# One-hots of 42 nodes a group in both graph layers, with three bf16 parts stacked in one contraction

## What is computed

```python
# layer 0, 4 heads of 32
xl = x @ W_lin.T;  x_j = xl[src]
alpha = leaky_relu((xl[dst]*att_src).sum + (x_j*att_dst).sum + (ef*att_edge).sum)
e = exp(alpha - segment_max(alpha, dst)[dst])
out = segment_sum(x_j * e / segment_sum(e, dst)[dst], dst) + bias + x
x = layernorm(x + elu(layernorm(out) * gamma + beta))
# layer 1, 8 heads of 16
q, k, v = x @ Wq.T, x @ Wk.T, x @ Wv.T
alpha = (q[dst] * w_ij * k[src]).sum(head) / 4 * cutoff
x = layernorm(x + segment_sum(alpha * v[src], dst))
```

## Time and profile before

| | |
|---|---|
| median of 3 runs | 4795.31 us |
| profiled execution | 4802.87 us |
| its span, first to last instruction | 4801.1 us |
| PE / PE weight loads | 49% / 45% busy |
| VectorE (DVE) | 51% |
| ScalarE (ACT) | 12% |
| GpSimd (POOL) | 75% |
| gathers of layer 0, first to last start | 46.2 to 2218.6 us |
| gathers of layer 1, first to last start | 2445.9 to 4744.5 us |
| data moved | 595.82 MB, mean 124 GB/s |

### The profile page before, as it was taken

How to read it: one execution, slowest core, us unless ns; L and a number is a source line. 1 busy time by engine, 2 the same in 40 slices (tenths; PEclk the granted TensorE clock), 3 DMA queues, 4 the chain that set the end, 5 groups by cost and what they waited for, 6 DMA issues and landing times. The chain is left out here.

```text
span 4801.1 us, 60860 instructions
## 1 busy us (share of the span) xinstructions
PE 2362.4 (49%) x18992; PEld 2166.5 (45%) x18992; DVE 2435.6 (51%) x3629; ACT 588.2 (12%) x893; POOL 3583.5 (75%) x3333
## 2 busy tenths in 40 slices
PE   2333334444444433335556555555555555556654
PEld 2333333333333333334345555555555555555553
DVE  2344444444444444445845555555555555555555
ACT  0111111111111111111420000000000000000002
POOL 5777777777777777773557777777777777777775
PEclk6666666666666666667677878888888787787786
DMA  7433333444444443332344444444444444444443
GB/s 166 104 103 103 100 101 101 109 111 111 111 111 111 107 112 102 101 102 54 107 148 145 142 146 142 146 141 147 143 145 144 143 146 142 146 141 147 141 146 94
DMA packets 324898, 595.82 MB, mean 124 GB/s; under 512 B 101041, under 2 KB 194257, under 8 KB 324593
## 3 DMA queue, kind: packets, MB, share of 16 engines
q0 software_dynamic: 130160, 323.05, 26.5%
q1 hardware_dynamic: 181424, 261.60, 17.1%
q10 hardware_dynamic: 13264, 10.66, 0.7%
HBM read 578.39 MB, written 16.64 MB: 124 GB/s over the span
## 5 line engine op out<-in xcount | busy, mean ns | idle before, releaser
L1157 POOL DMA_INDIRECT ring<-kv_table,den_cols x1616 | 1807.3, 1118 | 518.5 <-issue 518.2
L393 POOL DMA_INDIRECT ring<-x_table,idx x1612 | 1672.7, 1038 | 524.4 <-issue 491.1
L1197 PE MATMUL psum<-ring,work 128*128 128x128 f32 x3232 | 671.6, 393 | 925.0 <-DVE ring L1268 921.3
L1197 PEld LDWEIGHTS psum<-ring,work 128*128 128x128 f32 x3232 | 623.6, 296 | 967.6 <-issue 966.3
L1265 DVE TENSOR_TENSOR ring<-ring 128x1024 f32<-128x1024 f32 x202 | 247.5, 1225 | 871.3 <-POOLq L1169 871.3
L1204 PE MATMUL psum<-work,ring 128*128 128x128 f32 x3232 | 516.1, 327 | 39.7 <-DVE ring L1279 38.8
L1204 PEld LDWEIGHTS psum<-work,ring 128*128 128x128 f32 x3232 | 501.4, 244 | 55.0 <-DVE ring L1279 54.3
L482 PE MATMUL psum<-work 128*128 128x128 f32 x3232 | 490.5, 315 | 14.5 <-DVE work L676 14.5
L1240 ACT ACTIVATE work<-psum 128x1024 f32<-128x1024 f32 x202 | 206.9, 1024 | 2083.8 <-PE psum L1188 2083.8
L482 PEld LDWEIGHTS psum<-work 128*128 128x128 f32 x3232 | 452.6, 224 | 16.2 <-DVE work L676 16.1
L452 PE MATMUL psum<-ident_sb,score 128*128 128x128 f32 x51 | 15.5, 442 | 840.4 <-DVE score L599 840.4
(11 more groups left out here) (161 smaller groups left out, 2218.0 us busy)
## 6 DMA issues: line engine op xcount, KB each, us to landing
dst_all<-dst_row_dram SPq DMA_DIRECT2D x204, 512.0 KB
ring<-ea_dram SPq DMA_DIRECT2D x202, 512.0 KB, 4.0
ring<-kv_table,den_cols POOLq DMA_INDIRECT x1616, 2.9
ring<-x_table,idx POOLq DMA_INDIRECT x1612
ea_pair<-ea_turned_dram SPq DMA_DIRECT2D x102, 128.0 KB, 2.6
ring<-q_table SPq DMA_DIRECT2D x202, 64.0 KB, 1.8
ring<-xpad_dram SPq DMA_DIRECT2D x20, 320.0 KB, 3.4
kv_table<-ring ACTq DMA_DIRECT2D x10, 640.0 KB, 4.1
```

The costliest lines, as they stand in the source:

```text
L393: pool.indirect_dma_start(x_rows[:, h * CHUNK_TILES + t, :], None, k["x_table"], bass.IndirectOffsetOnAxis(idx[h][:, t:t + 1], 0))\
L1157: pool.indirect_dma_start(kv[j][:, t, :], None, k["kv_table"], bass.IndirectOffsetOnAxis(idx[:, tile:tile + 1], 0))\
L1197: last = pe.matmul(q_ps[j % 2][:, t * P:(t + 1) * P], onehotT[:, t * P:(t + 1) * P], q_win[j], start=True, stop=True)
```

## The change

The window of a pass is 42 nodes (`WIN`) in place of 128, so that three parts of each of 42 nodes fit on 126 partitions (`KWIN`).

- Both tables of target values are stored as (node, part, value) in bf16. 42 nodes are then 126 rows, and one bf16 product over 126 partitions adds the three parts. The turned one-hot repeats each node three times (`node_of` is `arange(128) // 3`).
- Layer 0 scores: 2 products of 512 columns a group into `dst_ps`, in which the group's four scores have rows of their own; at a chunk's end a ScalarE copy, 8 transposes and two more VectorE steps bring them to the edges' layout.
- Layer 0 denominators: fp32 products of `ex` with the fp32 one-hot. `ex_parts`, `ex_group`, `onehot_bf` and ScalarE's two copies a group go.
- Layer 1: the turned one-hot is made as in layer 0, from `dst_all` that SP loads; the 8 transposes (L1188), ScalarE's copy (L1240) and the fp32 spread go; the spread is 8 bf16 products.
- Operands move to PSUM: `iota_pass` and a copy of `ex` in layer 0; `iota_pass`, `alpha` and the intermediate product in layer 1, where q is now multiplied first.
- `q_table` is made on POOL (`split_q`, four instructions a batch) and written by SP.
- Each slot of `kv` has three semaphores in turn.

```diff
+WIN = 42
+KWIN = PARTS * WIN
...
-    q_table = nc.dram_tensor("q_table", [NODE_ROWS, FEAT], F32, kind="Internal").ap()
+    q_table = nc.dram_tensor("q_table", [NODE_ROWS, PARTS, FEAT], BF16, kind="Internal").ap()
...
+    iota_pass = k["bank"][3][:, 0:WIN]
+    ex_ps = k["bank"][3][:, P:P + HEADS0 * CHUNK_TILES].rearrange("p (h t) -> p h t", h=HEADS0)
...
             def scores_group(d, g):
...
-                for t in range(GROUP):
-                    at = (g * GROUP + t) * HEADS0
-                    for part in range(PARTS):
-                        last = pe.matmul(scores_ps[:, at:at + HEADS0], onehotT[g % 2][:, t * P:(t + 1) * P],
-                                         ai_win[g % 2][:, part * HEADS0:(part + 1) * HEADS0],
-                                         start=False, stop=False)
+                for half in range(2):
+                    last = pe.matmul(dst_ps[:, half * 512:(half + 1) * 512], ai_win[:, g * ROWS:(g + 1) * ROWS],
+                                     onehotT[g % 2][:, half * 512:(half + 1) * 512], start=False, stop=False)
...
+            def close_scores(s):
...
+                wait_here(pe, dst_copied, s + 1, pe_gate)
+                for t in range(GROUP):
+                    last = pe.transpose(dst_turned[:, t * ROWS:(t + 1) * ROWS], dst_scores[:, t * P:(t + 1) * P],
+                                        k["ident_sb"][0:ROWS, 0:ROWS])
...
             def make(u, s, tile):
-                dve.tensor_tensor(out=onehot[u], in0=k["iota_pass"].unsqueeze(1).to_broadcast([P, GROUP, P]),
+                dve.tensor_tensor(out=onehot[u], in0=iota_pass.unsqueeze(1).to_broadcast([P, GROUP, WIN]),
...
-                    in1=ex[:, :, bass.DynSlice(tile, GROUP)].rearrange("p h t -> p t h").unsqueeze(3)
+                    in1=ex_ps[:, :, bass.DynSlice(tile, GROUP)].rearrange("p h t -> p t h").unsqueeze(3)
...
+            def split_q(u, n):
+                q = qkv[u][:, :, 0:FEAT]
+                pool.wait_ge(qkv_copied, BATCH * (n + 1) + 2)
+                if n > 1:
+                    pool.wait_ge(q_out[u], 16 * (n // 2))
+                pool.tensor_copy(q_parts[u][:, :, 0, :], q)
+                for p in range(1, PARTS):
+                    pool.drain()
+                    last = pool.tensor_tensor(out=q if p < PARTS - 1 else q_parts[u][:, :, p, :], in0=q, in1=q_parts[u][:, :, p - 1, :],
+                                              op=ALU.subtract)
+                    if p < PARTS - 1:
+                        pool.drain()
+                        pool.tensor_copy(q_parts[u][:, :, p, :], q)
+                last.then_inc(q_split, 1)
...
+            for n in range(BATCHES - 2):
+                u = n % 2
+                first_power(n + 1)
+                second_power(u, n)
+                add_bias(u, n // 2 + 1)
+                take_one_off(u, n // 2 + 1)
+                if n:
+                    split_q(1 - u, n - 1)
             first_power(BATCHES - 1)
             second_power(0, BATCHES - 2)
+            split_q(1, BATCHES - 3)
             second_power(1, BATCHES - 1)
+            split_q(0, BATCHES - 2)
+            split_q(1, BATCHES - 1)
...
+                    sp.wait_ge(onehotT_made, n0 + j + 1)
+                    sp.dma_start(dst_all[j % 2], k["dst_row"][0:1, bass.DynSlice((SLOTS * i + j) * GP, GP)]
+                                 .to_broadcast([P, GP])).then_inc(dst_in[j % 2], 16)
                     sp.wait_ge(msg_made, n0 + j + 1)
-                    sp.dma_start(q_win[j], k["q_table"][bass.DynSlice(starts[j], P), :]).then_inc(q_in[j], 16)
+                    sp.dma_start(q_win[j], k["q_table"][bass.DynSlice(starts[j], WIN), :, :].rearrange("n s f -> (n s) f"))\
+                      .then_inc(q_in[j], 16)
...
+            def make_onehot(i, n, j):
+                dve.wait_ge(dst_in[j % 2], 8 * n + 16 - 8 * (j % 2))
+                dve.wait_ge(q_spread, n + 1)
+                dve.tensor_scalar(onehotT[j % 2], dst_all[j % 2][0:KWIN, :], k["base_f"][0:KWIN, bass.DynSlice(i, 1)],
+                                  k["node_pass"][0:KWIN, :], ALU.subtract, ALU.is_equal).then_inc(onehotT_made, 1)
+                dve.tensor_tensor(out=onehot[j], in0=iota_pass.unsqueeze(1).to_broadcast([P, GROUP, WIN]),
...
             def messages(i, n, j, nth):
-                dve.wait_ge(w_in[j], 16 * (nth + 1))
-                dve.wait_ge(kv_ready, n + 1)
-                dve.tensor_tensor(out=prod, in0=kv[j][:, :, 0:FEAT], in1=w[j], op=ALU.mult)
-                dve.drain()
-                dve.wait_ge(q_spread, n + 2)
-                dve.tensor_tensor(out=prod, in0=prod, in1=tiles3(q_ps[j % 2]), op=ALU.mult).then_inc(q_used, 1)
+                dve.wait_ge(kv_ready, n + 1)
+                dve.wait_ge(q_spread, n + 3)
+                q = tiles3(q_ps[j % 2])
+                dve.tensor_tensor(out=q, in0=q, in1=kv[j][:, :, 0:FEAT], op=ALU.mult)
+                dve.drain()
+                dve.wait_ge(w_in[j], 16 * (nth + 1))
+                dve.tensor_tensor(out=prod, in0=q, in1=w[j], op=ALU.mult).then_inc(q_used, 1)
```

More of the change, by code:

```diff
@@ L116, in program @@
     work = sb("work", [P, 5 * GROUP * P])
+    dst_all = [sb(f"dst_all{i}", [P, GROUP * P], I32) for i in range(2)]
     idx0 = [sb(f"idx{i}", [P, CHUNK_TILES], I32) for i in range(2)]
@@ L290, in layer0, with part @@
     GP = GROUP * P
[L291 to L295 removed]
+    cut = [0]
+    def part(cols):
+        cut[0] += cols
+        return k["work"][:, cut[0] - cols:cut[0]]
+    onehot = [part(GROUP * WIN).rearrange("p (t n) -> p t n", t=GROUP) for _ in range(2)]
+    message = [part(GP).rearrange("p (t f) -> p t f", t=GROUP) for _ in range(2)]
+    onehotT = [part(GP // 2).bitcast(BF16)[0:KWIN, :] for _ in range(2)]
+    ROWS = CHUNK_GROUPS * HEADS0
+    dst_scores = part(GP)[0:ROWS, :]
+    assert cut[0] <= 5 * GP
+    dst_all = k["dst_all"]
     ea_pair = [sb(f"ea_pair{i}", [P, 2, P]) for i in range(2)]
@@ L566, in next_pass @@
                 dve.drain()
-                for numbers in (k["node_pass"], k["iota_pass"]):
-                    dve.tensor_scalar(numbers, numbers, float(P), None, ALU.add)
+                for numbers in (k["node_pass"], iota_pass):
+                    dve.tensor_scalar(numbers, numbers, float(WIN), None, ALU.add)
                 dve.drain()
@@ L761, in between @@
     qkv = [part(3 * B).rearrange("p (b w) -> p b w", b=BATCH) for _ in range(2)]
+    q_parts = [part(3 * B // 2).bitcast(BF16).rearrange("p (b s w) -> p b s w", s=PARTS, b=BATCH) for _ in range(2)]
     rden = part(BATCH * HEADS0)
@@ L802, in between @@
     qkv_out = [S(f"qkv_out{i}") for i in range(2)]
+    q_split = S("q_split")
+    q_out = [S(f"q_out{i}") for i in range(2)]
     with nc.Block() as block:
@@ L1069, in layer1 @@
     w = [tiles3(part(GP)) for _ in range(SLOTS)]
-    q_win = [part(FEAT) for _ in range(SLOTS)]
+    q_win = [part(FEAT // 2).bitcast(BF16)[0:KWIN, :] for _ in range(SLOTS)]
     prod = tiles3(part(GP))
+    iota_pass = k["bank"][1][:, 0:WIN]
     message = [tiles3(part(GP)) for _ in range(2)]
     idx = k["idx1"]
-    alpha = part(GROUP * HEADS1)
+    alpha = k["bank"][1][:, P:P + GROUP * HEADS1]
     edge_w = part(GROUPS1 * GROUP)
     assert cut[0] <= RING_COLS - NODE_ROWS
-    onehot = [tiles3(k["work"][:, u * GP:(u + 1) * GP]) for u in range(SLOTS)]
-    onehotT = k["work"][:, 4 * GP:5 * GP]
-    sum_ps = [k["bank"][u][:, 0:P] for u in range(2)]
-    T_ps = k["wide"][0]
+    GW = GROUP * WIN
+    onehot = [tiles3(k["work"][:, u * GW:(u + 1) * GW]) for u in range(SLOTS)]
+    onehotT = [k["work"][:, SLOTS * GW + u * GP // 2:SLOTS * GW + (u + 1) * GP // 2].bitcast(BF16)[0:KWIN, :] for u in range(2)]
+    dst_all = k["dst_all"]
+    sum_ps = [k["wide"][0][:, u * 512:u * 512 + WIN] for u in range(2)]
     q_ps = [k["psum"][:, 2 * 512:4 * 512], k["wide"][1]]
@@ L1085, in layer1 @@
     idx_in = S("idx1_in")
-    kv_in = [S(f"kv_in{i}") for i in range(SLOTS)]
+    TURNS = 3
+    kv_in = [[S(f"kv_in{i}_{c}") for c in range(TURNS)] for i in range(SLOTS)]
     w_in = [S(f"w1_in{i}") for i in range(SLOTS)]
@@ L1096, in layer1 @@
     summed = S("summed1")
+    added = S("added1")
     pool_gate = S("pool1_gate")
@@ L1286, in add @@
                 dve.wait_ge(summed, n + 1)
-                window = k["sumT"][:, bass.DynSlice(start, P)]
-                dve.tensor_tensor(out=window, in0=window, in1=sum_ps[j % 2], op=ALU.add)
+                window = k["sumT"][:, bass.DynSlice(start, WIN)]
+                dve.tensor_tensor(out=window, in0=window, in1=sum_ps[j % 2], op=ALU.add).then_inc(added, 1)
             def one_round(i, groups, first, r):
@@ L1314, in _ @@
                 dve.drain()
-                dve.tensor_scalar(k["iota_pass"], k["iota_pass"], float(P), None, ALU.add)
+                for numbers in (k["node_pass"], iota_pass):
+                    dve.tensor_scalar(numbers, numbers, float(WIN), None, ALU.add)
                 dve.drain()
```

264 lines of the change are left out of this document (122 added, 142 removed).

## The result

The changed kernel takes 4518.77 us (median of 4 runs, 4516.26 to 4521.41) where the kernel before takes 4795.03: a ratio of 0.9424, 95% interval 0.9408 to 0.9440. It is faster by 276 us; forecast were 308.

What follows compares the result with a forecast made beforehand. The prediction took POOL, busy with gathers, as the bound. Its terms gave a span of 4801.1 - 249 - 110 - 5 + 56 = 4493 us, then 4493 + 1.8 - 7.6 = 4487 us, range 4400 to 4600 us.

Steps and rivals of the forecast that it cites:

- POOL is the bound, and its gathers' excess is on the path: Both layers: POOL goes from gather to gather; gather time above the median, 274 and 146 us, is all on the path.
- What holds a gather is VectorE's second SBUF input: Both layers: gathers wait for VectorE instructions reading two SBUF tensors; one input in PSUM frees them, -274 and -146 us.
- The slower rival: Both layers: any VectorE work holds gathers, so the 420 us stay and the time is 4846 us; chance 0.05.
- the -110: Layer 0: -146 us from L673 and L676 no longer holding gathers, +36 us for holds that stay.
- The turned one-hot holds for 0.56 us, met 45% of the time: 25 + 36 us: Holds left at random phase: 25 us in layer 1; 36 in layer 0, of which 11 are for the maxima.
- Gathers land late: Layer 1: extra loads delay gathers' landing past 6 us, so POOL stands 0.5 us a group, 4588 us; chance 0.05.
- The ring between the layers: Between the layers: POOL's split waits for ScalarE's table copies, making a step 18.4 us against 12.3; +56 us (37 to 80).
- After the last gather VectorE sets the time: After layer 0's last gather: casts go, a second `ex` copy is added, ten groups of sums change by -2; sum -5 us.
- From the span to the median: Whole kernel: the profiled execution is 1.8 us over its span and 7.6 over the median, so 4493 becomes 4487 us.

Runs made afterwards that it cites:

- b_q_first_2: Kernel before with only layer 1's product order changed, kv times q first, in place in PSUM, then times w: 4700.55 us, ratio 0.9803.
- a_no_hold_2: Changed kernel with both layers' turned one-hots made by a scalar_tensor_tensor that reads the node numbers from PSUM: 4462.06 us, ratio 0.9310.
- a_all_sbuf: Changed kernel with one-hot node numbers, layer 0's exponentials and layer 1's weights back in SBUF, q product still first and in PSUM: 4679.19 us, ratio 0.9763.
- a_same: The changed kernel, unaltered, run again on the second chip beside its variants: 4517.73 us, ratio 0.9427.

## Why the prediction was right, by its steps

**POOL is the bound, and its gathers' excess is on the path.** Right, but for one reading: not all idle time before the gathers of before was "issue". In layer 0 33 us of 524 were waits for VectorE, and 31 still are. The sum of the gathers' durations fell by 1807.3 - 1566.3 = 241 us in layer 1 and 1672.7 - 1571.0 = 102 us in layer 0, and the layers' stretches by 232 and 102.

**What holds a gather is VectorE's second SBUF input.** Right for the `tensor_tensor` instructions, and shown by two runs that move operands alone: one product reordered -93 us, the operands put back +160 us. The turned one-hot holds with a single tensor in SBUF (beside its two columns of scalars); in another form and with the node column in PSUM it holds nothing, -56 us. The slower rival, VectorE at work at all, would have had `b_q_first_2` at no gain and `a_no_hold_2`, whose VectorE works longer, at a loss. Where the account falls short is layer 0: the prediction puts its gain down to L673 and L676 losing one SBUF input, and gives the shorter one-hot nothing. The -102 us are near the -110, but with both inputs back in SBUF (`a_all_sbuf`) only 18 of them are lost. That the two numbers agree is partly luck: the step holds for 18 us, and the rest came with other parts of the change.

**The turned one-hot holds for 0.56 us, met 45% of the time: 25 + 36 us.** A little small. Above the medians now stand 1566.3 - 1616 x 0.946 = 37.6 us in layer 1 and 1571.0 - 1612 x 0.944 = 49.3 us in layer 0. When a gather is held is more involved than one hold from 0.25 us on. In layer 1 there are four cases, by when the gather asks: from 0.28 us before the start of L1293 to 0.10 after it, 51 gathers wait until 0.11 us after the start, 11 us in sum; from 0.11 to 0.27 us, 38 pay nothing; from 0.27 us to near the end, 82 wait for its end, 25 us; and 31 meet the end of one that had been stretched, 0.08 us each, 2 us. Inside L1293 162 gathers ask, 28 us in sum, 0.137 us a group against the 0.125 of a random phase; the 11 us of those that ask before its start had no place in the prediction. This varies from one execution to the next: in `a_same` the 28 us are 18. In layer 0 L590 takes 26 us and the maxima's scans and adds 18 us, against 25 and 11.

By the Trainium skill (SBUF — State Buffer, § Who interferes with whom) an instruction in a two-port mode holds the shared ports for its whole length. The row of 331.75 in the earlier trace rows and the cases above show otherwise: 38 gathers ask 0.11 to 0.27 us after the start and pay nothing. The same section says that a DMA which seems stalled by VectorE is one for which GpSimd is kept from generating descriptors; that fits what these gathers show, in that POOL's own instruction becomes longer, but no run tells what part of its work is held up.

**Gathers land late.** A rival at 0.05, and a small part of it came: POOL's gaps in layer 1 sum to 501 instead of 492 us, 13 of them over 0.6 us, and the gather of 3009.09 above has a DMA as what ended the idle time before it. 9 us instead of the rival's 101, at a DMA share of 0.65 where I gave 0.69.

**The ring between the layers: +6.1 us for 8 steps, +7 at the end, 56 in all.** The ring is there, every step of it in the order that was given, but shorter. In the batch shown it takes 8.8 us from the end of a second power (2232.41) to the end of the last table copy (2241.20; forecast 10.1), 4.7 for the split (5.6) and 2.7 for the two powers (2.7); the eight steps with a split are 16.6 us long on average, against 18.4. From the first second power to the last it is +38 us, from there to the first gather +2, against +49 and +7. By the Trainium skill (GPSIMD Engine Reference, § 3.1) the estimate was 4.7 us a split, of 1.39 us for each two-input instruction and 0.96 for each cast. The rows of L883 show 1.39; the cast takes 0.72, less than that. (With 4.7 us a split the term of 56 us comes to 47, not 46.)

**After the last gather VectorE sets the time, -5 us.** This step failed. It is TensorE. Stretches of the last chunk's sums, before and after, in the columns of the earlier trace rows:

```profile
2240.00:2300.00 60.00, 37.82 (x285) 33.74 (x285) 36.90 (x64) 16.27 (x26) 6.80 (x7) 0.78 0.12 35
```

```profile
2140.00:2190.00 50.00, 47.94 (x320) 45.61 (x320) 17.85 (x41) 0.62 (x1) 0.14 (x2) 0.50 0.00 1
```

```profile
2140.07 3.64 PE L505 MATMUL psum<-work 128*128 128x42 f32 x16 [3.30 <-DVE work L687]
2143.64 1.28 PE L507 MATMUL psum<-work,score 128*4 128x42 f32 x16
2144.86 3.64 PE L505 MATMUL psum<-work 128*128 128x42 f32 x16
2148.43 1.28 PE L507 MATMUL psum<-work,score 128*4 128x42 f32 x16
```

TensorE works 47.94 of 50 us, at the clock 0.50, 4.8 us a group; before, the clock of these 60 us was 0.78 in the mean, but nine of the ten groups ran at 1.00, the higher level of 2.4 GHz: there the 16 message products of three times the columns took 2.05 us, and a group 3.5.

```profile
2250.52 2.05 PE L482 MATMUL psum<-work 128*128 128x128 f32 x16 [0.54 <-DVE work L676]
```

From the first group's add to the last one's it is 43.1 us for 31.2, and VectorE waits 29 us of the 50 for TensorE's sums. I had the fp32 denominators in the sum, but at the clock of before. From the last gather to the first second power it is 104.6 instead of 93.0 us: +11.6, not -5. That the stretch came out at +51.3 as forecast is luck, two errors that cancel: 17 us too little here, 16 too much in the ring and its end.

**From the span to the median.** The profiled execution of before lay 7.6 us above the median and I carried that over; that of after lies 0.1 below its own. So of the 32 us between 4487 and 4519, 24 are the terms above (17 in layer 1, 8 in layer 0, -2 at the start, +1 at the end), and 7.6 are this.

What stays open: whether SP's queue is what keeps the nine steps between the layers above 108 us when the split is moved or shortened, what part of the change brings most of layer 0's gain, what it is in the turned one-hot that holds a gather, and what starves the engines on the first chip.

## What to carry to other kernels

Where POOL issues indirect DMAs without a break, compare their mean with their minimum: in this kernel most of the excess was time in which a VectorE instruction with two SBUF inputs ran, and in layer 1 one operand in PSUM gave it back, with no instruction fewer. Where two such instructions stand back to back, as in layer 0, shortening the first may do as much; undo the parts one at a time before you say which it was. An engine that waits in a queue ahead of the next batch's first step makes a ring of what were two pipelines; put such work a step later. And before a stretch is given to one engine, work it out at the clock that the change may bring, not at that of before.

## What the runs showed of the hardware that I had not expected

- TensorE's granted clock fell from 0.67 and 0.80 in the two stretches to 0.50, with its busy time in the first up (161 to 276 us of 400) and in the second down (293 to 225 us of 500). The message products are a third as wide and there are a third fewer matmuls in the stretch of layer 1; which of these goes with the clock no run separates.
- A third of the columns takes 3% less time at the same clock: 16 products of 42 columns take 3.64 us at 0.50, 16 of 128 columns took 3.76 where the kernel before had 0.50, and 2.03 at 1.00. The 16 weight loads beside them take 3.49 us at 0.50 in both kernels and 1.86 at 1.00, so the time goes with them and not with the columns.
- A `tensor_scalar` of 0.81 us lets a gather through that asks 0.11 to 0.27 us after its start, and grows by that to 0.87 us at most. One that asks 0.52 to 0.30 us before its start pays nothing either and stretches it to as much as 1.03 us. One that asks between these two groups, from 0.28 us before the start to 0.10 after it, is held until 0.11 us after the start.
- On one chip the kernel before took 6100 us. Of the four variants that were traced there, three of the changed kernel and one of the kernel before, all show whole engines that wait some 2 us or more from one instruction to the next in stretches. The three variants of the changed kernel were slower than the kernel before there, and the two of them that ran elsewhere were 6 to 7% faster.
